# A four-layer network on one core: semaphores cleared inside the next norm, query weights loaded a layer early, loops over batches written out, all fetches of the sparse experts first

## The reference

```python
x = L0_attn_x                                     # [4, 512, 128]
x = _layernorm(x + _L0_attn_ref(x, ...))          # softmax attention, 16 heads, rotary and ALiBi
x = _layernorm(x + _L0_ffn_ref(x, ...))           # gated MLP, 512 hidden, two hidden layers more
x = _layernorm(x + _L1_attn_ref(x, ...))          # selective scan, both gates, own norm
x = _layernorm(x + _L1_ffn_ref(x, ...))           # MoE, 8 experts, top 2, capacity 320
x = _layernorm(x + _L2_attn_ref(x, ...))          # queries and keys of 8 heads, softmax over the queries
x = _layernorm(x + _L2_ffn_ref(x, ...))           # 32 sparse experts, top 2, cap 80, 16 adapters
x = _layernorm(x + _L3_attn_ref(x, ...))          # rotary attention, 16 heads
x = _layernorm(x + _L3_ffn_ref(x, ...))           # 8 experts that choose 4096 (expert, token) pairs, shared expert
```

```python
xe = xf[idx]                                       # [32, 80, 128]: the 80 rows of each expert
gate, upv = jnp.split(jnp.einsum('eci,eji->ecj', xe, w_up), 2, axis=-1)
ye = jnp.einsum('ecj,eoj->eco', jax.nn.silu(gate) * upv, w_down)
out = jnp.zeros((T, C)).at[idx.reshape(-1)].add((w[..., None] * ye).reshape(-1, C))
...
vals, idx = jax.lax.top_k(scores.reshape(-1), S * 2)   # choice: best S*2 of all scores
h = jax.nn.gelu(jnp.einsum('sd,edf->esf', xf, W1) + b1[:, None, :], approximate=True)
y = jnp.einsum('esf,efd->esd', h, W2) + b2[:, None, :]
```

## Time and profile before

| | before |
|---|---|
| median of three runs | 1896.82 us (1896.57 to 1897.28) |
| profiled execution | 1899.36 us |
| its span, first to last instruction | 1897.6 us |
| mean granted TensorE clock | 0.903 |
| instructions | 22237 |
| TensorE matmul busy | 1541.0 us (81%) |
| VectorE, ScalarE, GpSimd busy | 1039.2, 924.2, 411.2 us |

### The profile page before, as it was taken

The page is one execution under the profiler, slowest core; times in us unless marked ns, Lnnn a source line. Parts: engine busy times, 40 slices in busy tenths (PEclk is TensorE's granted clock), DMA queues, the critical chain, the costliest instruction groups (busy, mean ns, idle before and its releaser), DMA issues. The chain is left out here.

```text
span 1897.6 us, 22237 instructions
## 1 busy us (share of the span) xinstructions
PE 1541.0 (81%) x7296; PEld 664.5 (35%) x7296; DVE 1039.2 (55%) x2156; ACT 924.2 (49%) x1578; POOL 411.2 (22%) x370
## 2 busy tenths in 40 slices
PE   4699998899848898779799870674899977699997
PEld 1244443343302333234233430672122223344443
DVE  8577772100006999947577649423888825433332
ACT  4766665432257887520166640222477762234343
POOL 4101100000027898700022200560121100000000
PEclk7799998999958999989799985796699997899999
DMA  5112200100000000000111091013121102000000
GB/s 141 43 33 54 60 19 7 56 0 0 19 9 1 5 5 5 1 30 1 35 29 40 1 361 46 18 21 126 59 69 60 35 21 85 6 1 0 0 0 22
DMA packets 51965, 72.21 MB, mean 38 GB/s; under 512 B 11442, under 2 KB 44490, under 8 KB 50103
## 3 DMA queue, kind: packets, MB, share of 16 engines
q1 hardware_dynamic: 49814, 69.20, 12.0%
q0 software_dynamic: 2048, 1.73, 0.5%
HBM read 48.29 MB, written 18.12 MB: 35 GB/s over the span
## 5 line engine op out<-in xcount | busy, mean ns | idle before, releaser
L656 ACT ACTIVATE a_probs_sb<-a_t_ps 128x512 f32<-128x512 f32 x512 | 286.7, 596 | 129.3 <-PE a_t_ps L537 72.8
L747 DVE CUSTOM_DVE_ANT_0 a_biased<-a_s_ps,a_bias 128x512 f32<-128x512 f32 x256 | 166.2, 686 | 67.8 <-issue 67.6
L533 PE MATMUL a_t_ps<-a_stack 126*128 126x512 bf16 (+1 forms) x512 | 169.6, 395 | 30.4 <-DMA a_stack<-a_least_parts 11.7
L514 PE MATMUL a_s_ps<-a_stack 96*128 96x512 bf16 (+1 forms) x512 | 155.4, 412 | 39.4 <-DMA a_stack<-a_stacks 25.3
L1429 DVE TENSOR_TENSOR_SCAN s_h<-s_dA,s_dbu 128x1024 f32<-128x1024 f32 x64 | 146.6, 2290 | 52.9 <-POOL s_dbu L1394 44.3
L754 DVE TENSOR_REDUCE a_least_sb<-a_s_ps 128x2 f32<-128x1024 f32 x128 | 152.7, 1220 | 34.4 <-PE a_s_ps L514 34.1
L1394 POOL TENSOR_TENSOR s_dbu<-s_du,s_bs 128x1024 f32<-128x1024 f32 x64 | 152.3, 2391 | 29.5 <-DVE s_h L1429 27.9
L2843 ACT ACTIVATE c_hid<-c_up_ps,c_b 128x512 f32<-128x512 f32 x128 | 87.9, 687 | 143.6 <-PE c_up_ps L2812 143.6
L2853 DVE TENSOR_TENSOR c_gated_sb<-c_hid,c_g_ps 128x2048 f32<-128x2048 f32 x32 | 73.2, 2288 | 146.4 <-ACT c_hid L2843 146.4
L552 PE MATMUL a_o_ps<-a_probs_sb,a_vpad 128*16 128x512 f32 x1024 | 138.7, 615 | 0.2 <-ACT a_probs_sb L656 0.2
L2812 PE MATMUL c_up_ps<-xT,c_w 128*128 x256 | 118.0, 605 | 6.0 <-DMA c_select<-in_c_select 6.0
(11 more groups left out here) (452 smaller groups left out, 2539.9 us busy)
## 6 DMA issues: line engine op xcount, KB each, us to landing
x_wu<-in_x_wu SPq DMA_DIRECT2D x2, 4096.0 KB, 17.9
a_stacks<-a_p SPq DMA_DIRECT2D x16, 384.0 KB, 3.0
a_stack<-a_stacks SPq DMA_DIRECT2D x32, 192.0 KB, 3.9
a_stack<-a_stacks SPq DMA_DIRECT2D x64, 96.0 KB, 2.3
a_stacks<-a_p SPq DMA_DIRECT2D x16, 256.0 KB, 2.4
q_q<-q_q SPq DMA_DIRECT2D x32, 128.0 KB, 2.3
x_wd<-in_x_wd SPq DMA_DIRECT2D x2, 2048.0 KB, 33.5
c_w<-in_c_w SPq DMA_DIRECT2D x2, 2048.0 KB, 10.6
```

What stands on the lines that cost most here:

```text
L514: made = nc.tensor.matmul(s_ps[:, 2 * (x % 2) + e, :], operand(0, k, pair, e, SCORE_ROWS)[:, t * P:(t + 1) * P], operand(1, k, pair, e, SC ...
L533: last = nc.tensor.matmul(out, operand(1, k, pair, e, TURNED_ROWS)[:, t * P:(t + 1) * P], operand(0, k, pair, e, TURNED_ROWS), start=True, ...
L656: nc.scalar.activation(probs[:, y % PROB_RING, e, :], bank("turned", y, e), ACT.Exp, scale=-1.0).then_inc(probs_ready, 1)
L747: nc.vector.tensor_tensor_reduce(out=biased[:, e, :], in0=s_ps[:, 2 * (x % 2) + e, :], in1=bias[:, h, at:at + N], scale=1.0, scalar=3.0e38 ...
```

## The change

1. START is gone. All semaphores begin at zero; waits for zero are left out (`wait`), and with them go the nops and the barriers in front of them.
2. The block with the clears is gone. A stage's semaphores are held until the next `layernorm_stage`, whose block has a GpSimd part that clears them. The semaphores of choice are cleared in last_ln.
3. MoE and query softmax become one stage; its weights are loaded in m_ln, behind the MoE's.
4. The loops over batches of the gated MLP, `choice_route` and `choice_experts` are written out. DVE's search stays a loop.
5. Sparse experts: `got` and `results` have a place for each of the 32 experts. All fetches are issued first (fetch e waits until fetch e - 4 has landed), then all scatters. ACT and DVE are loops now: the first and the last turn written out, six turns between, each of two pairs; addresses of `results`, `got` and the waited-for values come from registers. `weigh` is done for two experts at a time. Ten semaphores still begin at START, by nops in the block of the sparse route.

```diff
-            self.nc.all_engine_barrier()
         return self.nc.Block()
-    def run_stage(self, stage, *args):
-        self.stage_sems = []
-        with ExitStack() as self.stage_ctx:
+    def clear_stale(self, pool):
+        for handle in self.stale_flags:
+            pool.sem_clear(handle)
+        self.stale_flags = []
+
+    def run_stages(self, stages, *args):
+        stale_ctx = ExitStack()
+        for stage in stages:
+            self.stage_ctx, self.stage_flags = ExitStack(), []
             stage(self, *args)
-            with self.nc.Block() as block:
-                @block.gpsimd
-                def _(pool):
-                    for handle in self.stage_sems:
-                        pool.sem_clear(handle)
+            stale_ctx.close()
+            stale_ctx, self.stale_flags = self.stage_ctx, self.stage_flags
...
+def wait(engine, semaphore, value):
+    if value > 0:
+        engine.wait_ge(semaphore, value)
...
+        @block.gpsimd
+        def _(pool):
+            core.clear_stale(pool)
...
+            def load_weights(sp):
...
+                query.load(sp, A)
...
+        query_softmax(core, xT, query)
...
-            with pe.Fori(0, B - 1) as i:
+            for i in range(B - 1):
                 first(i)
                 up(i + 1)
                 second_and_out(i)
...
-        got = core.sb(mem, "x_got", [CAP, X_RING, X_ROW])
+        got = core.sb(mem, "x_got", [CAP, E, X_ROW])
...
+        def run(engine, body):
+
+            body(0)
+            with engine.Fori(1, TURNS - 1) as i:
+                body(i)
+            body(TURNS - 1)
...
             def fetch(e):
-                if e >= X_RING:
-                    pool.wait_ge(turned, (e - X_RING) // PAIR + 1)
-                    pool.wait_ge(weighed, (e - X_RING) // SOME + 1)
+                if e >= SOME:
+                    pool.wait_ge(fetched[e % SOME], 16 * (e // SOME))
...
-            for e in range(X_RING):
+            for e in range(E):
                 fetch(e)
             for e in range(E):
-                if e + X_RING < E:
-                    fetch(e + X_RING)
                 scatter(e)
...
+            run(act, experts)
...
+            run(dve, experts)
...
-            with pe.Fori(0, B) as i:
+            for i in range(B):
                 def up(e):
```

More of the change, by code:

```diff
@@ new lines, in experts @@
+            def experts(i):
+                for u in range(UNITS):
+                    up(i, u)
+                    if u == 0:
+                        turn(i, 1)
+                    if u == PAIR + 1 and not (isinstance(i, int) and i == TURNS - 1):
+                        turn(i + 1, 0)
+                    if u > 0:
+                        down(i, u - 1)
+                    elif not (isinstance(i, int) and i == 0):
+                        down(i - 1, UNITS - 1)
+            turn(0, 0)
@@ L2413, in _ @@
+            pe.wait_ge(w_loaded, 16 * 8)
+            for i in range(TURNS):
+                experts(i)
+            down(TURNS - 1, UNITS - 1)
             for i in range(B):
@@ new lines, in result, with experts @@
+                wait(act, down_ready, e + 1)
+                wait(act, weighed, g + 1)
+                nc.scalar.activation(one(results, e), d_ps[kind - 1][0:CAP, 0:C], ACT.Copy,
+                                     scale=weight[:, 0, PAIR * a + kind - 1:PAIR * a + kind]).then_inc(result_ready, 1)
+            def experts(i):
+                for u in range(UNITS):
+                    n = UNITS * i + u
+                    wait(act, up_ready, n + 1)
+                    wait(act, act_ready, n - 1)
+                    nc.scalar.activation(silu[:, u % 2, :], up_ps[u % 3][:, 0:PAIR * CAP], ACT.Silu) \
+                        .then_inc(silu_ready, 1)
+                    if u >= 2:
+                        result(i, u - 2)
+                    elif not (isinstance(i, int) and i == 0):
+                        result(i - 1, UNITS + u - 2)
@@ L2490, in _ @@
+            keep(0, 0)
+            run(dve, experts)
             for i in range(B):
```

566 lines of the change are left out of this document (270 added, 296 removed).

## The result

| | before | after |
|---|---|---|
| median | 1897.05 us (4 runs, 1896.57 to 1897.42) | 1842.66 us (4 runs, 1841.46 to 1843.40) |
| ratio of the two, 95% interval | | 0.9713 (0.9696 to 0.9730) |
| span of the profiled execution | 1897.6 us | 1839.6 us |
| mean granted TensorE clock | 0.903 | 0.916 |

On the chip of one set of experiments (its kernel before took 1918.6 us), and again of the last two runs (1914.6), every program took 15 to 40 us more, nearly all of it in one place of the sparse experts; of those runs only the other stages are read.

What follows compares the result with a forecast made beforehand. The prediction took engines standing still for bookkeeping at stage boundaries as the bound. Gaps 21.6, query 5.6, starts 3.7, loops 0.3, sparse experts 3.0 and clock 2.3 sum to 36.5 us: 1860 us, forecast 1856 to 1865, wider range 1852 to 1869.

Steps and rivals of the forecast that it cites:

- The gaps: Ahead of the seven norms: gaps with clears shrink to 0.30 us each, 21.6 us saved, plus 0.7 at program start.
- the query's: Between MoE and query block: early weight loads and no clears cut the 5.89 us gap to 0.30, 5.6 us saved.
- the other starts: Nops and barriers removed before choice_route 1.8, choice_experts 0.8 and the store 0.33 us.
- What it is worth: TensorE clock: c_ln and last_ln start fast, 6.9 slow us at 0.33 each, 2.3 us; nothing for f_ln, m_ln, a_ln.
- begins before the norm: m_ln: its slow clock time begins at 824.2, before the norm, so no clock gain was counted there.
- the clock gives more: Rival, chance 0.12: f_ln, m_ln and a_ln also start at the upper clock, sparse reaches 4.4; 1852 to 1856 us.
- between 0 and 3 x 0.39 = 1.2 us ... I take 0.3: Gated MLP: writing out the loops removes back edges of 0.39 us in three turns; 0.3 us saved.
- Sparse experts: Sparse experts: all fetches first puts the last scatter's issue at 1274.7 instead of 1277.54; 3.0 us gained.
- 0.45 us a pair: Sparse experts: cost of ACT's and DVE's loops with register addresses, 0.15 us a unit, a third of the bound.
- The bound of 4.4: Sparse experts: the most that can be won, 4.4 us, with fetches at 1.21 and scatters at 1.24 us.

Runs made afterwards that it cites:

- own_clears: Changed kernel with each stage's clears put back into a block of their own behind the stage: 1864.03 us, ratio 0.9834.
- gap25: Changed kernel with a block ahead of each of the seven norms in which GpSimd clears one unused semaphore 25 times: 1871.09 us, ratio 0.9857.
- gap55: Changed kernel with a block ahead of each of the seven norms in which GpSimd clears one unused semaphore 55 times: 1883.42 us, ratio 0.9924.
- choice_starts: Changed kernel with 20 nops and a barrier back ahead of choice_route, 7 nops and a barrier ahead of choice_experts: 1847.40 us, ratio 0.9741.
- choice_loops: Changed kernel with hardware loops back in the shared expert and choice experts, turns 1 to 3: 315.16 us from c_ln's first matmul to last_ln's.
- sparse_ring_2: Changed kernel with the sparse experts of the kernel before (ring of 8, fetches and scatters by turns), second run: 1844.02 us, ratio 0.9710.
- sparse_straight: Changed kernel with ACT's and DVE's loops in the sparse experts written out, all fetches still first: ratio 0.9713.
- best: Changed kernel with c_select and c_b2 loaded in c_ln, norms' ACT tables loaded ahead of the barrier: ratio 0.9785 first, 1840.03 us second.
- q_late: Changed kernel with the three query weight loads back at the head of the query block: ratio 0.9823 first, 1846.78 us second.
- own_clears_again: Second execution of the changed kernel with the stages' clears in their own blocks, on another chip than the first: 1903.5 us.
- before_again: Second execution of the unchanged kernel before, on another chip than the first: 1911.5 us.

## Why the prediction was wrong

The direction and the boundaries were right. The gaps came to 22.2 us where the sum had 22.3, the query's to 5.6 for 5.6, the other starts to 3.5 for 2.9 (choice_experts gave 1.4 for 0.8); own_clears put 20.6 us of gaps back, and its time rose by 19.6. Three terms of the sum were mis-sized. By the medians they make the 18 us: about 12 in the clock, 3.6 in the loops of the MLP, 2.0 in the sparse experts.

**Clock.** The step "What it is worth", 2.3 us with 0 for f_ln, m_ln and a_ln, failed. The first pair of traces has 17.8 us there, the medians leave about 14, and 10 to 12 us come again in the second pair. The largest part of these is m_ln with its router, 4.4 us, where I counted nothing: I had argued that its low clock "begins before the norm" and so stays, and it went in every run with the short gap (12.33 us for 16.75). ssm and x_ln with the sparse route, 1.6 each, were counted at nothing as well. For f_ln it was right to count nothing: its 4.2 us are luck of the two executions, and the second ones have 0.04. The price was too low as well: 0.33 us for each us at the lower level came from two norms cut by hand, while f_ln's stretch has it at 4.2 us for 0.28 of 15.79 x 2, or 8.8 us: 0.48. And of the two norms that I counted on, last_ln gave 1.5 us for the 1.1 forecast, and c_ln kept its low clock: its own work took as long as before.

What is shown of the cause is less than the whole. That gaps ahead of a norm can bring the lower clock back is shown by gap25 and gap55, 13.5 and 10.9 us beyond the gaps, by own_clears at last_ln (1.5 us) and m_ln (1.6 of the 4.4), and by choice_starts, 0.9 beyond its own. That the length of the gap doesn't settle it is shown by m_ln in own_clears and gap25. The clears' gaps, the nops of choice and the late query loads together bring back some 6 us (4.5, 0.9 and 0.5); what gave the rest of the 10 to 14 is open, since no run puts all gaps of the kernel before back at once. My rival "the clock gives more" named m_ln rightly and f_ln and a_ln beside it, for which two executions don't agree, and stopped at 6 to 7 us.

**Loops of the MLP.** The step "between 0 and 3 x 0.39 = 1.2 us ... I take 0.3" looked at back edges. The loops' price was a table load behind a wait, 1.0 to 1.3 us a turn; 3.9 in the traces, 3.0 reproduced by the late load alone, 0 by the loops alone. The rule on branches that speaks for unrolling ("Runtime: NRT & Kernel Launch" of the Trainium skill, section "Instruction fetch mechanics") would have put the gain at the branches. The two runs with the MLP's loops put back, and choice_loops at 315.16 for 315.03, show none there; whether a branch of theirs led outside the code held, as the rule supposes, no run shows.

**Sparse experts.** Forecast 3.0, measured 5.0 in the stage (with 1.6 to 2.9 of it seen in the whole time of sparse_ring_2). The sum had 1277.54 - 1274.7 = 2.8, rounded up, not down, to 3.0. The estimate of 0.45 us a pair for the loops' registers was about right (4.15 for 3.83 is 0.32), but it was on no path: at 4.15 us a pair GpSimd still sets the end, and sparse_straight, at 3.83, ends at the same time. The bound of 4.4 was 0.6 short since the scatters come at 1.22 us, not 1.24.

What held: GpSimd's clears hid in the norms, none of which grew; the early query loads delayed nothing in the MoE (88.2 us from m_ln's first matmul to the query block's with them, 88.2 without them when the longer gap is taken off); no cost of the nops in the sparse route showed.

What stays open: why the clock falls in one gap and not in another of the same length, and which of the changes gave the rest of the clock's share.

## What to carry to other kernels

An idle TensorE can cost more than the idle time. Gaps of 2 us ahead of seven norms cost as much again in clock behind them (gap25), while gaps of 1 to 4 us from the clears cost between nothing and a quarter more (own_clears). So a saving at a boundary should be priced with the clock of the work behind it as a range, from a stretch of the same work at each level.

Compare two executions before a stretch is explained. f_ln differed by 4.2 us in the first pair of traces and by 0.04 in the second; m_ln by 4.4 in both.

Look at what a wait is tied to. A table load, or anything that needs no data, should stand ahead of the wait for data. In the hardware loop whose counts began at 1 the load stood behind it, and that, not the branch, was the loop's price; in the loop whose counts began at zero it did not.

Where one engine's issue is back to back (GpSimd's 64 DMAs at 1.21 us), only its count and its start mattered; loops or straight code on the others were free.

## What was not expected of the hardware

On the chip of the third set ACT stood still in the sparse experts with its inputs there. ACT's silus in the kernel best on that chip:

```profile
1177.49 0.30 ACT L2456 ACTIVATE x_silu_sb<-x_up_ps 128x160 f32<-128x160 f32 x1 [4.60 <-PE x_up_ps L2395]
1197.20 0.30 ACT L2456 ACTIVATE x_silu_sb<-x_up_ps 128x160 f32<-128x160 f32 x1 [19.40 <-remote]
...
1209.93 0.30 ACT L2456 ACTIVATE x_silu_sb<-x_up_ps 128x160 f32<-128x160 f32 x1 [12.17 <-remote]
```

The second and third wait 19.40 and 12.17 us, while the matmuls that they read had, by the order of the program, ended by 1177 and 1182 (TensorE itself is idle for 28.71 us there), and GpSimd goes on issuing fetches every 1.21 us. Three other kernels with all fetches first (q_late, choice_loops, own_clears_again) have TensorE idle for 27.5, 29.9 and 29.7 us in the same place; with the ring it was spread in waits of 3 to 5 us (22 us in all in before_again). The kernel before took 1918.6 us there, and the ratios of the four kernels lie at 0.976 to 0.982. For the three with all fetches first this is 16 to 19 us more than the same edits cost on an undisturbed chip, for the ring 9. So the change seems to be worth less on such a chip, by an estimate of 16 to 19 us; the changed kernel itself was not run there. What ACT waited for isn't shown by the trace, and no experiment was made on it.
